# Remainders and clamp off VectorE, du*B for two units at once, TensorE's tasks behind every second spread

## The reference

```python
xz = einsum('gld,ed->gle', x, in_proj_w);  xi, z = split(xz, 2)
u = silu(causal_conv4(xi) + conv_b)
dt, Bm, Cm = split(einsum('gld,ed->gle', u, x_proj_w), [1, 17])
delta = softplus(dt * dt_proj_w + dt_proj_b);  A = -exp(A_log)
def step(h, (d_t, u_t, B_t, C_t)):
    h = h * exp(d_t[..., None] * A) + (d_t * u_t)[..., None] * B_t[:, None, :]
    return h, einsum('gdn,gn->gd', h, C_t)
y = (scan(step) + u * D) * silu(z)
out = einsum('gld,ed->gle', y, out_proj_w)
```

## Time and profile before

| | us |
|---|---|
| median of 3 runs | 9622.17 (9618.43 to 9636.53) |
| profiled execution, span from first to last instruction | 9611.3 |
| VectorE busy | 7428.8 (77%) |
| TensorE busy | 7650.9 (80%) |
| GpSimd busy | 5297.9 (55%) |
| ScalarE busy | 5208.4 (54%) |

### The profile page before, as it was taken

The page is one execution under the profiler, slowest core; times in us unless marked ns, Lnnn a source line. Parts: engine busy times, 40 slices in busy tenths (PEclk is TensorE's granted clock), DMA queues, the critical chain, the costliest instruction groups (busy, mean ns, idle before and its releaser), DMA issues. The chain is left out here.

```text
span 9611.3 us, 134613 instructions
## 1 busy us (share of the span) xinstructions
PE 7650.9 (80%) x30601; PEld 4061.9 (42%) x30601; DVE 7428.8 (77%) x10037; ACT 5208.4 (54%) x9100; POOL 5297.9 (55%) x4494
## 2 busy tenths in 40 slices
PE   9977777777777777777777777777778999999996
PEld 9952222222222222222222222222224799959996
DVE  7759999999999999999999999999994122211222
ACT  0236766767666676666767676676761133301332
POOL 0008888788887878788888788878882000000000
PEclk9988888888788888888878887878888999999998
DMA  9655555655556566565566566556552000040002
GB/s 175 168 126 157 159 159 158 160 155 163 155 158 159 156 160 157 157 159 158 160 156 159 155 158 160 155 159 158 158 160 80 28 0 0 0 98 3 0 0 53
DMA packets 1108327, 1201.90 MB, mean 125 GB/s; under 512 B 460432, under 2 KB 1094800, under 8 KB 1107344
## 3 DMA queue, kind: packets, MB, share of 16 engines
q1 hardware_dynamic: 871568, 1117.24, 44.4%
q10 hardware_dynamic: 236032, 77.08, 3.5%
HBM read 961.04 MB, written 155.41 MB: 116 GB/s over the span
## 5 line engine op out<-in xcount | busy, mean ns | idle before, releaser
L640 POOL TENSOR_TENSOR prod<-hs,bsp 128x448 f32<-128x448 f32 x3584 | 4272.7, 1208 | 1221.6 <-DVE hs L628 891.3
L628 DVE TENSOR_TENSOR_SCAN hs<-da,hs,ps 128x448 f32<-128x448 f32 x3072 | 3475.0, 1131 | 0.0
L603 PE MATMUL ps<-stack,seld 96*128 96x448 bf16 x3587 | 1465.4, 414 | 1587.8 <-DVE hs L628 1548.1
L619 DVE TENSOR_TENSOR ps<-ps,bsp 128x448 f32<-128x448 f32 x3585 | 2178.1, 608 | 39.1 <-PE ps L603 25.4
L609 ACT ACTIVATE da<-da,nega 128x448 f32<-128x448 f32 x3588 | 2190.9, 661 | 23.0 <-issue 20.4
L603 PEld LDWEIGHTS ps<-stack,seld 96*128 96x128 bf16 x3587 | 355.6, 99 | 3332.1 <-DVE hs L628 3064.4
L902 PE MATMUL ps<-pv,ws 128*128 128x224 f32 x8800 | 1692.3, 354 | 9.4 <-ACT pv L1057 7.1
L902 PEld LDWEIGHTS ps<-pv,ws 128*128 128x128 f32 x8800 | 1657.1, 188 | 45.2 <-issue 7.8
L651 PE MATMUL ps<-prod,wc 128*32 128x448 f32 x7200 | 1407.0, 744 | 13.9 <-POOL prod L640 13.6
L1239 DVE SCALAR_TENSOR_TENSOR pv<-ps,R 128x224 f32<-128x224 f32 x880 | 422.1, 480 | 1279.4 <-PE ps L902 1279.4
L407 PE MATMUL ps<-xn,wtap 128*128 128x448 f32 x1808 | 1019.3, 671 | 1.6 <-ACT bsp L467 1.6
(11 more groups left out here) (118 smaller groups left out, 7491.7 us busy)
## 6 DMA issues: line engine op xcount, KB each, us to landing
da<-delta_copy SPq DMA_DIRECT2D x3595, 224.0 KB, 3.7
stack<-parts SPq DMA_DIRECT2D x2700, 28.0 KB, 2.3
delta_copy<-dlt SPq DMA_DIRECT2D x225, 224.0 KB, 1.9
lnx<-in_x SPq DMA_DIRECT2D x118, 224.0 KB, 3.7
lny<-y_nchw SPq DMA_DIRECT2D x118, 224.0 KB, 4.4
x_column_pairs<-otile SPq DMA_DIRECT2D x225, 116.0 KB, 2.7
xpad<-x_column_pairs SPq DMA_DIRECT2D x32, 812.0 KB, 4.4
xpad<-in_x SPq DMA_DIRECT2D x64, 392.0 KB, 6.6
```

Source lines behind the costliest of these rows:

```text
L603: pe.matmul(ps[:, DU_BANK + j % 4, 0:T], seld[0:96, b, :], stack[:, st.t % 2, grp, :], start=True, stop=True).then_inc(S["du_spread"], 1)
L619: v.tensor_tensor(du, du, bsp[:, st.t % 2, 0, :], ALU.mult).then_inc(S["dbu_done"], 1)
L628: v.tensor_tensor_scan(hs[:, j, :], da[:, j % SLOTS, :], ps[:, DU_BANK + j % 4, 0:T], 0.0 if first else hs[:, j, T - 1:T], ALU.mult, ALU.add)\
L640: g.tensor_tensor(prod[:, j % 8, :], hs[:, j, :], bsp[:, st.t % 2, 1, :], ALU.mult)\
```

## The change

VectorE loses three operations a tile. rest0 and rest1 go to GpSimd, behind its products of steps 1 and 4. The clamp min(log + e - q, e) is written as e - relu(q - log): GpSimd makes q - log (`delta_over`, step 9), ScalarE the relu (`clamp_over`, step 13), GpSimd the difference and the sum with relu(v) (`delta_sum`, step 12), then delta*u (step 13).

VectorE's drive takes two PSUM banks in one instruction, with B read twice, and stands behind the scan of every even unit, two units ahead. So it waits for the second of two spreads.

TensorE's tasks stand behind even steps only. ScalarE's cast1 moves from step 6 to step 4, ahead of the silu table load and `u`. SP's order is unchanged.

```diff
-PE_AT = {0: ["tap0"], 1: ["last3", "tap1"], 2: ["tap2", "tap3"], 3: ["z"], 4: ["project"], 5: ["lnc"], 6: ["bc0"],
-         7: ["dt"], 8: ["sum0", "bc1"], 9: ["lnv"], 11: ["sum1"], 14: ["sum2"]}
-ACT_AT = {2: ["relu", "cast0"], 5: ["silu", "u", "z", "exp"], 6: ["evacuate", "cast1"], 7: ["lnc"], 8: ["bc0"],
-          9: ["dt"], 10: ["dt2", "bc1"], 11: ["lnv"], 14: ["shift"]}
-DVE_AT = {0: ["add_x"], 2: ["rest0"], 3: ["gate"], 6: ["rest1"], 11: ["scale"], 14: ["min"]}
-POOL_AT = {11: ["delta_log"], 14: ["delta_u"]}
+PE_AT = {0: ["tap0"], 2: ["last3", "tap1", "tap2"], 4: ["tap3", "z", "project"], 6: ["lnc", "bc0"],
+         8: ["dt", "sum0", "bc1"], 10: ["lnv"], 12: ["sum1"], 14: ["sum2"]}
+ACT_AT = {2: ["relu", "cast0"], 4: ["cast1"], 5: ["silu", "u", "z", "exp"], 6: ["evacuate"], 7: ["lnc"], 8: ["bc0"],
+          9: ["dt"], 10: ["dt2", "bc1"], 11: ["lnv"], 13: ["clamp"], 14: ["shift"]}
+DVE_AT = {0: ["add_x"], 3: ["gate"], 11: ["scale"]}
+POOL_AT = {1: ["rest0"], 4: ["rest1"], 9: ["over"], 12: ["delta"], 13: ["delta_u"]}
-LEAD = {"du": 3, "decay": 4, "drive": 1, "load": 11}
+LEAD = {"du": 3, "decay": 4, "drive": 2, "load": 11}
...
+        def delta_over(g, st):
+            g.wait_ge(S["d_q"], st.far + 1)
+            g.tensor_tensor(ds2[:, :], dq[:, :], dln[:, :], ALU.subtract).then_inc(S["d_over"], 1)
+        def clamp_over(a, st):
+            a.wait_ge(S["d_over"], st.far + 1)
+            a.activation(ds2[:, :], ds2[:, :], ACT.Relu).then_inc(S["d_clamp"], 1)
+        def delta_sum(g, st):
+            g.wait_ge(S["d_clamp"], st.far + 1)
+            g.tensor_tensor(ds1[:, :], dexp[:, :], ds2[:, :], ALU.subtract).then_inc(S["d_log"], 1)
...
+            g.wait_ge(S["d_log"], st.far + 1)
+            g.tensor_tensor(dlt[:, 0, :], ds1[:, :], drelu[:, :], ALU.add).then_inc(S["delta"], 1)
...
-        def rest_of(v, st, part):
+        def rest_of(g, st, part):
...
         def drive(v, st, j):
             n = st.tile * UN + j
-            v.wait_ge(S["du_spread"], n + 2)
+            v.wait_ge(S["du_spread"], n + 3)
...
-            du = ps[:, DU_BANK + j % 4, 0:T]
-            v.tensor_tensor(du, du, bsp[:, st.t % 2, 0, :], ALU.mult).then_inc(S["dbu_done"], 1)
+            b = DU_BANK + j % 4
+            du = ps[:, b:b + 2, 0:T]
+            v.tensor_tensor(du, du, bsp[:, st.t % 2, 0:1, :].to_broadcast([P, 2, T]), ALU.mult)\
+                .then_inc(S["dbu_done"], 1)
         def scan(v, st, j):
-            v.wait_ge(S["dbu_done"], n + 3)
+            v.wait_ge(S["dbu_done"], st.tile * (UN // 2) + (j // 2 + 2))
...
                     for j in range(UN):
-                        drive(v, *unit(st, j + LEAD["drive"]))
                         scan(v, st, j)
+                        if j % 2 == 0:
+                            drive(v, *unit(st, j + LEAD["drive"]))
```

More of the change, by code:

```diff
@@ L188, in build @@
             "tmp_done", "u_ready", "sz_ready", "d_abs", "d_relu", "d_exp", "d_ln", "d_w", "d_q",
-            "d_s1", "d_s2", "d_min", "delta", "delta_u",
+            "d_over", "d_clamp", "d_log", "delta", "delta_u",
             "cast", "rest", "split", "stacked",
@@ L512, in ln_shift @@
             a.activation(xn[:, k:k + T], xg[:, :], ACT.Identity, bias=vec_c(1)).then_inc(S["xn_ready"], 1)
-        def delta_log(g, st):
+        def delta_over(g, st):
             if not (st.ahead and st.k == 0):
@@ L531, in delta_times_u @@
                 g.sem_inc(S["gates"], 1)
+            g.wait_ge(S["d_log"], st.far + 1)
+            g.tensor_tensor(dlt[:, 0, :], ds1[:, :], drelu[:, :], ALU.add).then_inc(S["delta"], 1)
+        def delta_times_u(g, st):
+            if not (st.ahead and st.k == 0):
                 g.wait_ge(S["split"], st.far)
                 g.sem_inc(S["gates"], 1)
-            g.wait_ge(S["d_min"], st.far + 1)
-            g.tensor_tensor(dlt[:, 0, :], ds1[:, :], drelu[:, :], ALU.add).then_inc(S["delta"], 1)
+            g.wait_ge(S["u_ready"], st.far + 1)
+            g.sem_inc(S["gates"], 1)
             g.wait_ge(S["delta"], st.far + 1)
-            g.sem_inc(S["gates"], 1)
-            g.wait_ge(S["u_ready"], st.far + 1)
             g.tensor_tensor(dlt[:, 1, :], dlt[:, 0, :], u[:, st.far_u, :], ALU.mult).then_inc(S["delta_u"], 1)
@@ L551, in cast_part @@
             a.copy(parts[:, part, :], src).then_inc(S["cast"], 1)
-        def rest_of(v, st, part):
-            v.wait_ge(S["cast"], st.next * 2 + part + 1)
+        def rest_of(g, st, part):
+            g.wait_ge(S["cast"], st.next * 2 + part + 1)
             if part == 0:
-                v.tensor_tensor(rest[:, :], dlt[:, 1, :], parts[:, 0, :], ALU.subtract).then_inc(S["rest"], 1)
+                g.tensor_tensor(rest[:, :], dlt[:, 1, :], parts[:, 0, :], ALU.subtract).then_inc(S["rest"], 1)
             else:
-                v.tensor_tensor(parts[:, 2, :], rest[:, :], parts[:, 1, :], ALU.subtract).then_inc(S["split"], 1)
+                g.tensor_tensor(parts[:, 2, :], rest[:, :], parts[:, 1, :], ALU.subtract).then_inc(S["split"], 1)
         def stack_part(sp, st, part):
@@ L980, in _ @@
                 act_task(a, st, "dt2")
+                clamp_over(a, st)
                 if k == 0:
@@ L1001, in _ @@
                                 cast_part(a, st, int(name[4]))
+                            elif name == "clamp":
+                                clamp_over(a, st)
                             elif name == "evacuate":
@@ L1103, in _ @@
             v.sem_inc(S["exp_done"], 2)
-            v.sem_inc(S["dbu_done"], 2)
+            v.sem_inc(S["dbu_done"], 1)
             v.sem_inc(S["scan_done"], 8)
@@ L1114, in _ @@
                 ln_scale(v, st)
[L1115 to L1121, removed]
+            drive(v, Step(0, 0), 0)
             with v.Fori(0, PAIRS) as p:
@@ L1126, in _ @@
                     for j in range(UN):
-                        drive(v, *unit(st, j + LEAD["drive"]))
                         scan(v, st, j)
+                        if j % 2 == 0:
+                            drive(v, *unit(st, j + LEAD["drive"]))
                         for name in DVE_AT.get(j, ()):
-                            if name == "min":
-                                delta_min(v, st)
-                            elif name == "gate":
+                            if name == "gate":
                                 gate(v, tile, ub)
-                            elif name.startswith("rest"):
-                                rest_of(v, st, int(name[4]))
                             elif name == "add_x":
@@ L1257, in _ @@
             st = Ahead(0)
-            delta_log(g, st)
+            delta_over(g, st)
+            delta_sum(g, st)
             delta_times_u(g, st)
-            delta_log(g, Ahead(1))
+            delta_over(g, Ahead(1))
+            delta_sum(g, Ahead(1))
+            for part in range(2):
+                rest_of(g, st, part)
             delta_times_u(g, Ahead(1))
@@ L1267, in _ @@
                         for name in POOL_AT.get(j, ()):
-                            if name == "delta_log":
-                                delta_log(g, st)
+                            if name == "over":
+                                delta_over(g, st)
+                            elif name == "delta":
+                                delta_sum(g, st)
+                            elif name == "delta_u":
+                                delta_times_u(g, st)
                             else:
-                                delta_times_u(g, st)
+                                rest_of(g, st, int(name[4]))
             barrier(g, 3)
```

## The result

The changed kernel takes 9512.9 us (median of 4 runs, 9504.9 to 9523.6) where the kernel before takes 9620.3 us beside it: a ratio of 0.9883, 95% interval 0.9869 to 0.9897. It is faster by 107 us; 322 were forecast.

A forecast was written before the change was run, and what follows sets the result against it. VectorE, 98% busy, set 29.25 us a tile; afterwards loops through u would set 27.8 (27.3 + 0.5 for low clock). Saving 1.45 us x 224 = 325 us from 9622 gave 9300 us (55%), range 8980 to 9530.

The forecast's parts named there:

- VectorE's own sum: Scan stage: VectorE alone would need 29.25 - 2.18 - 0.25 = 26.8 us a tile, present short waits included.
- The double drive: VectorE: one drive of 896 elements takes 1.07 us, saving 0.03 us a pair, 0.25 us a tile.
- GpSimd's prices: GpSimd: 1.09 us an operation, rest0 and rest1 included; 22 operations take 24.0 us a tile.
- the rival on bf16 operands: rest0 and rest1 dear on GpSimd: at three times 1.09 us, 30.0 us a tile, 9790 us; 8%.
- The loop over rest0 and cast1: From u through dq, GpSimd's operations, rest0, ScalarE's cast1 and table load to u: 26.5 us without layer norm, mean 27.3.
- The tiles with layer norm: Half of the tiles: the loop from u through GpSimd and cast1 back to u takes 28.2 us there.
- present short waits stay: VectorE in the scan stage: its short waits remain unchanged inside the 26.8 us a tile.
- TensorE at half clock: Slot 2 (last3, two taps) takes 4.7 us at low clock; assumed for half of the tiles, adding 0.5 us.
- its own loop: TensorE: u to dq, GpSimd steps, slot 2 at half clock, spreads, tap3, u: 27.5 us without layer norm.
- Slot 8 just fits: TensorE's dt, skip, bc1 and sum0 take some 3.2 us; any overrun falls on VectorE, with 1.0 us to spare.

The follow-up runs named there:

- the second experiment: Changed kernel with TensorE's slot 8 cut to sum0 then dt, and bc1 moved to slot 10: 9616.8 us, ratio 1.0002 to the kernel before.
- the single drives: Changed kernel with the drive part undone, one drive one unit ahead in front of each scan: 9506.9 us, ratio 0.9864 to the kernel before.

## Why the prediction was wrong

- **VectorE's own sum: right.** From 2000 to 6000 us its waits are 354 us in all; without them it needs 26.3 us a tile. The forecast's 26.8 holds 0.5 us of present waits, so it says 26.3 too.
- **The double drive: right** in size (1.08 us, 0.24 us a tile where it counts). The estimate worked out from the Trainium skill ("VectorE: DVE Perf Modes", the section on the TRN2 errata), 1.26 us a tile, was not seen.
- **GpSimd's prices: right.** rest0 and rest1 take 1.04 us; the rival on bf16 operands falls.
- **The loop over rest0 and cast1: right, for most tiles without layer norm.** 26.5 us were forecast for this kind. From the u of one such tile to the u of the next it is 26.56 us in the changed kernel in 66 of 90 cases, in which u does not wait for tap3, and the run without cast1's move shows that it is this loop. In the other 24 cases u waits for tap3, and it is 27.4 us. That the mean by scan starts, 26.45, comes so near is partly luck: it mixes the two, and over the seven tiles in a row u falls some 2 us back behind the scans, which is paid in the next tile with layer norm.
- **The tiles with layer norm: wrong**, 28.2 us forecast (29.2 with the low clock), 31.07 measured. The step that failed is the sentence that VectorE's "present short waits stay". The scale's wait for xrstd was 0.38 us a tile of this kind before. u moved back, behind cast1 and behind tap3 at slot 4, while VectorE came to the scale sooner, having lost its rests and a part of the drives. ScalarE's 12.9 us from u to xrstd became part of a loop of 30.6 us that no term of the sum held. The two layer-norm operations that the prediction left as they were changed as well, and nearly cancel: add_x went from 791 ns to 1293, scale from 1168 to 762.
- **TensorE at half clock: right in kind.** The clock in the stage was 0.79, and slot 2 lay in the low stretch in the tile shown. Without layer norm its own loop was sized well, 27.5 us for the 27.4 measured, but for half of the tiles where it held 24 cases of 90 (tap1 and tap2 take 3.0 to 3.4 us in these and 1.6 to 2.5 in the others). With layer norm it was priced in the wrong loop: u waits for tap3 in 93 of 104 such tiles, and what that delays is xrstd. "Slot 8 just fits" was wrong there too, as dt waits 0.8 us for xsq; by the second experiment and the single drives that stall alone cost nothing.
- In sum: with half of the tiles at the low clock 27.0 us without and 28.7 us with layer norm were forecast. The first came out 0.55 us better, the second 2.37 us worse: (2.37 - 0.55) x 112 = 204 us of the miss of 213.

## What to carry to other kernels

When work leaves the engine that sets the pace, write down for each kind of iteration every loop that closes over one iteration, with the short waits of the profile as the first candidates: a wait of 0.4 us before marks a chain that already ends last at that place, so that time saved ahead of it can come back as a longer wait. A mean over two kinds of tile hides that one gets worse. And an edit can be worth nothing until another loop is opened: cast1's place and the double drive moved nothing in the changed kernel, and some 180 and 88 us together with the others.

## What the runs showed of the hardware

- A GpSimd tensor_tensor of 448 elements with a bf16 operand takes 1.04 us where the all-f32 one takes 1.13 to 1.16 us in the same trace.
- Extra matmuls paid for themselves: 18 a tile raised the granted clock of the stage from 0.79 to 0.96, and a kernel in which they are the only edit to the changed one is 1.1% faster, though in 47 of 105 tiles without layer norm the low clock moved to slot 8. The Trainium skill ("TensorE: Matmul & The Clock Gate", Part 1) has it that the throttled state is the default and that activity releases it; this run agrees (0.79 to 0.96).
- VectorE's layer-norm sum (add_x), with two SBUF inputs, takes the longer the more of GpSimd's running operation is left when it starts: 0.66 to 0.68 us where none is running (4 tiles of the two kernels), 0.78 us with 0.2 to 0.4 us left (75 tiles before), 1.39 us with 0.8 to 1.0 us left (79 tiles after). The change moved its place beside GpSimd's products. The gate, with one input in PSUM, stays at 0.59 to 0.63 us in both. The Trainium skill ("GPSIMD Engine Reference", section 1) names operations of VectorE with two SBUF inputs as those that contend with GpSimd; the trace agrees.
